# First token chunk's attention output: sums loaded and inverted during groups 10 to 15, projected inside group 15

## The reference

```python
x = x + attn(layernorm(x), wq, wk, wv, wo)
x = x + ffn(layernorm(x), w_router, wg, wu, wd, sg, su, sd)
# attn: 32 query heads of 8, 8 key/value heads; a band of 128 keys below
# the diagonal is masked; softmax over all 1024 keys; out @ wo
# ffn: 8 experts of inner size 640, top 2 per token by sigmoid scores,
# and 2 shared experts of the same size that every token passes
```

## Time and profile before

| what | value |
|---|---|
| median of 3 runs | 960.42 us (959.5 to 963.53) |
| the profiled execution's own time | 959.4 us |
| its span | 957.7 us |
| TensorE busy | 897.4 us (94%) |
| ScalarE busy | 592.1 us (62%) |
| VectorE busy | 445.7 us (47%) |
| chain that ended last | TensorE 75%, ScalarE 9%, VectorE 6% |

### The profile page before, as it was taken

One profiled execution on the slowest core, in us unless ns is written; L12 is line 12 of the kernel. 1 busy time (PEld: TensorE's weight loads), 2 busy tenths in 40 slices (PEclk: granted clock), 3 DMA queues, 4 the chain that ended last, 5 costly groups with the idle time before them and its releaser, 6 DMA issues.

```text
span 957.7 us, 24218 instructions
## 1 busy us (share of the span) xinstructions
PE 897.4 (94%) x8205; PEld 570.2 (60%) x8206; DVE 445.7 (47%) x761; ACT 592.1 (62%) x736; POOL 275.3 (29%) x420
## 2 busy tenths in 40 slices
PE   6959999999999999999997999999999999999994
PEld 4523333333333333333346888888887888888883
DVE  5733334434443344444356767656653434334332
ACT  5769999999999999999982423342212222222221
POOL 4303333232333323333340000000012555444442
PEclk7979999999999999999997999999999999999998
DMA  4350555554444555532112207100027773565421
GB/s 139 105 174 35 179 206 203 196 191 167 148 167 157 205 205 202 196 95 88 31 50 71 66 1 253 38 8 23 1 75 264 259 210 90 160 165 142 143 38 22
DMA packets 41951, 123.67 MB, mean 129 GB/s; under 512 B 7608, under 2 KB 22968, under 8 KB 35760
## 3 DMA queue, kind: packets, MB, share of 16 engines
q1 hardware_dynamic: 30144, 109.37, 33.0%
q0 software_dynamic: 7008, 9.70, 5.7%
q10 hardware_dynamic: 4752, 4.01, 1.3%
HBM read 74.03 MB, written 49.02 MB: 128 GB/s over the span
## 4 chain that ended last, share of the span: by engine, by line
PE 75%; ACT 9%; DVE 6%; issue 5%; SPq 3%; DMA 1%; DVEq 0%; POOL 0%; POOLq 0%; ACTq 0%
PE ps L1618 17%; PE ps L1766 14%; PE ps L1571 13%; PE ps L1720 11%; ACT arena L920 7%; PE ps L1785 7%; PE ps L1733 5%; DVE ps L1118 3%; PE ps L1776 2%; PE ps L1671 1%; PE ps L1525 1%; SPq L529 1%; SPq L526 1%; PE ps L1747 1%; PE ps L1707 1%
## 5 line engine op out<-in xcount | busy, mean ns | idle before, releaser
L920 ACT ACTIVATE arena<-ps 128x1024 f32<-128x1024 f32 x336 | 317.0, 1044 | 5.3 <-PE ps L1571 5.3
L1618 PE MATMUL ps<-arena 128*32 128x256 f32 x4096 | 265.0, 385 | 0.1
L753 POOL TENSOR_SCALAR_AFFINE_SELECT arena<-arena 128x512 f32<-128x512 f32 x240 | 150.0, 638 | 302.0 <-ACT arena L931 202.4
L1571 PE MATMUL ps<-arena 64*128 64x512 bf16 (+1 forms) x1280 | 184.6, 342 | 20.6 <-SPq L568 6.2
L1618 PEld LDWEIGHTS ps<-arena 128*32 128x32 f32 x4096 | 111.8, 109 | 102.9 <-issue 38.2
L1118 DVE COPY_PREDICATED ps<-keep,ps 128x512 f32<-128x512 int32 (+1 forms) x128 | 80.5, 629 | 170.7 <-PE ps L1571 170.7
L1571 PEld LDWEIGHTS ps<-arena 64*128 64x128 bf16 x1280 | 53.6, 94 | 174.7 <-ACT arena L920 83.4
L1766 PE MATMUL ps<-wr_all,x2T 128*128 x648 | 145.7, 366 | 5.5 <-issue 3.5
L1766 PEld LDWEIGHTS ps<-wr_all,x2T 128*128 128x128 f32 x648 | 106.6, 190 | 27.6 <-issue 12.8
L1720 PE MATMUL ps<-x2T,wr_all 128*128 128x512 f32 x480 | 118.5, 398 | 1.2 <-issue 1.2
L931 ACT ACTIVATE arena<-ps 128x1024 f32<-128x1024 f32 x112 | 114.3, 1034 | 8.4 <-DVE ps L1118 3.6
(11 more groups left out here) (188 smaller groups left out, 731.6 us busy)
## 6 DMA issues: line engine op xcount, KB each, us to landing
w_scr<-wr_all SPq DMA_DIRECT2D x24, 1280.0 KB, 7.0
wr_all<-w_scr SPq DMA_DIRECT2D x24, 1280.0 KB, 5.7
raw<-w_experts SPq DMA_DIRECT2D x24, 640.0 KB, 7.1
arena<-q_scr SPq DMA_DIRECT2D x64, 64.0 KB
o_scr<-arena SPq DMA_DIRECT2D x128, 32.0 KB, 1.6
arena<-o_scr SPq DMA_DIRECT2D x16, 256.0 KB, 4.2
raw<-w_shared SPq DMA_DIRECT2D x6, 640.0 KB, 4.4
arena<-q_scr SPq DMA_DIRECT2D x32, 96.0 KB
```

Of the source, the lines that this page charges most:

```text
L753: nc.gpsimd.affine_select(out=dst, in_=src, compare_op=ALU.is_ge if own else ALU.is_gt, fill=0.0, base=0, pattern=[[0, REP], [-1 if own el ...
L920: nc.scalar.activation(prob[:, SLOT[unit(a, kt)], :, :].rearrange("p h q -> p (h q)"), score.rearrange("p b x -> p (b x)"), ACT.Exp, scale ...
L1571: return nc.tensor.matmul(ps[:, bank, :].rearrange("p (h q) -> p h q", h=2)[:, :, place * P:(place + tiles) * P], kst[r0:r0 + HALF, s, kt ...
L1618: last = nc.tensor.matmul(ps[32 * h:32 * h + 32, 6 + qc, a % 2 * QW:(a % 2 + 1) * QW], vst[:, s, kt, :], prob[:, SLOT[k], h, :], start=(no ...
```

## The change

`load_sums(0)` is issued after SP's part of group 10. Piece i of the inversion is put into VectorE's group 11 + i, between `merge_pair` 1 and `merge_pair` 2, and `normalize(0)` into group 15 at the same place. TensorE projects the first half of chunk 0 after score blocks 26 and 27 of group 15, into bank 6, and the second half after block 28, into the banks that block 26 has left; the value blocks of the last turns come behind. VectorE adds and takes each half's statistics as it comes, and writes the normalized rows to `xnc_first`, a place in the buffer that held the attention weights. The transposed rows of chunk 0 go to banks 4 and 5.

```diff
+XT_BANK = (4, 6, 6, 6)
+FIRST_O = (6, 2 * BUF[NEXP - 3])
...
@@ SP @@
-            for n in range(2 * LOOPED, NG - 1):
-                group_io(n, n % 2, n < SPLIT_PAIRS, n + 1 < NG - 1, n + 2 < NG)
-
...
-            sp.wait_ge(o_stored[0], 16 * REP * KV + FIRST)
-            load_sums(0)
-            group_io(NG - 1, 1, False, False, False)
+            for n in range(2 * LOOPED, NG):
+                group_io(n, n % 2, n < SPLIT_PAIRS, n + 1 < NG - 1, n + 2 < NG)
+                if n == 2 * LOOPED:
+                    sp.wait_ge(o_stored[0], 16 * REP * KV + FIRST)
+                    load_sums(0)
...
@@ VectorE @@
-            def group(g, s, more):
+            def group(g, s, more, also=lambda: None):
 
                 merge_pair(g, 1)
+                also()
                 merge_pair(g, 2)
...
+            for n in range(2 * LOOPED, NG - 1):
+                i = n - 2 * LOOPED - 1
+                group(n, n % 2, n + 2 < NG, (lambda: invert(0, i)) if 0 <= i < INVERT else (lambda: None))
+
+            def add_first(half):
+
+                dve.wait_ge(c_proj, half + 1 + FIRST)
+                for t in range(2 * half, 2 * half + 2):
+                    nc.vector.tensor_tensor(x_rows(0, t), x_rows(0, t), ps[:, FIRST_O[half], t % 2 * D:(t % 2 + 1) * D],
+                                            ALU.add) \
+                        .then_inc(c_added, 1)
+                for t in range(2 * half, 2 * half + 2):
+                    dve.wait_ge(c_added, t + 1)
+                    nc.vector.bn_stats(stats[:, t, :], x_rows(0, t)).then_inc(dve_step, 1)
+
+            def first_rows():
+
+                layernorm(dve, lambda t: x_rows(0, t), lambda t: xnc_first[:, t, :], first_base, INVERT, c_xn, NC + 1, False)
...
             merge_pair(NG - 1, 1)
-            invert(0, 0)
-            invert(0, 1)
+            normalize(0)
             merge_pair(NG - 1, 2)
             acc_out(NG - 1, 0)
             merge_pair(NG - 1, 3)
-            invert(0, 2)
-            invert(0, 3)
-            normalize(0)
+            add_first(0)
+            add_first(1)
+            first_rows()
             acc_out(NG - 1, 1)
-            new_rows(0)
             xT_copy(0)
             ahead_of(-1)
...
@@ TensorE @@
-            for t in range(1, len(TURNS)):
-                turn_of(NG - 1, 1, NG // 2 - 1, t, True, False)
-            for v in TURNS[0][1]:
-                if len(v) == 3:
-                    values(NG - 1, 1, unit(*v[0:2]))
-            pe.wait_ge(acc_free, 2 + NG * QC - 1)
...
+            LAST_MERGE = max(t for t, (products, _) in enumerate(TURNS) if (QP - 1, 1) in products)
+            last = (NG - 1, 1, NG // 2 - 1)
+            for t in range(1, LAST_MERGE + 2):
+                turn_of(*last, t, True, False)
+            products_of(*last, LAST_MERGE + 2, False)
+            pe.wait_ge(c_oT, 1)
+            pe.wait_ge(merged, NG * NMERGE)
+            project(0, range(0, 2))
+            products_of(*last, LAST_MERGE + 3, False)
+            pe.wait_ge(s_free, NG * NEXP - 2 + BUFS)
+            project(0, range(2, 4))
+            for t in range(LAST_MERGE + 2, len(TURNS)):
+                if t > LAST_MERGE + 3:
+                    products_of(*last, t, False)
+                values_of(*last, t, True)
+            for v in TURNS[0][1]:
+                if len(v) == 3:
+                    values(NG - 1, 1, unit(*v[0:2]))
```

More of the change, by code:

```diff
@@ L355, in build @@
         raw = at("raw", [P, 2, BW], F32, 2 * WSLOT + top[0])
+        xnc_first = arena[:, top[0]:top[0] + TPC * D].rearrange("p (t d) -> p t d", d=D)
+        assert top[0] + TPC * D <= 2 * WSLOT
         carve(2 * BW)
@@ L417, in build @@
         y_free, now_ix = sem("y_free"), sem("now_ix")
+        c_added = sem("c_added")
         shift_low, shift_high = sem("shift_low"), sem("shift_high")
@@ L442, in wait_apart, with layernorm @@
             eng.sem_inc(apart, 1)
-        def layernorm(eng, src, dst, base, n0, xn_done, round_):
+        def layernorm(eng, src, dst, base, n0, xn_done, round_, sums=True):
             n = n0
             for t in range(TPC):
-                nc.vector.bn_stats(stats[:, t, :], src(t)).then_inc(dve_step, 1)
+                if sums:
+                    nc.vector.bn_stats(stats[:, t, :], src(t)).then_inc(dve_step, 1)
                 n += 1
@@ L936, in x2_out @@
                 for k in range(KD):
-                    nc.scalar.copy(x2T[:, 0, k, ds(c * CT, CT)], ps[:, 6 + k, :]).then_inc(c_xT, 1)
-                act.dma_start(xn_scr[ds(c * CT, CT), :].rearrange("(t p) d -> p t d", p=P), xnc).then_inc(c_kept, 16)
+                    nc.scalar.copy(x2T[:, 0, k, ds(c * CT, CT)], ps[:, XT_BANK[c] + k, :]).then_inc(c_xT, 1)
+                act.dma_start(xn_scr[ds(c * CT, CT), :].rearrange("(t p) d -> p t d", p=P), xnc if c else xnc_first) \
+                    .then_inc(c_kept, 16)
             def shared(c):
@@ L1162, in _ @@
                     group(it * 2 + s, s, True)
-            for n in range(2 * LOOPED, NG - 1):
-                group(n, n % 2, n + 2 < NG)
             def x_rows(c, t):
@@ L1180, in normalize @@
             def normalize(c):
-                dve.wait_ge(dve_step, c * C_DVE + (first_base + INVERT))
+                dve.wait_ge(dve_step, c * C_DVE + (first_base - (TPC if c else 0) + INVERT))
                 nc.vector.tensor_tensor(numer, numer, denom, ALU.mult).then_inc(c_oT, 1)
+            for n in range(2 * LOOPED, NG - 1):
+                i = n - 2 * LOOPED - 1
+                group(n, n % 2, n + 2 < NG, (lambda: invert(0, i)) if 0 <= i < INVERT else (lambda: None))
+            assert NG - 2 * LOOPED - 2 == INVERT
+            def add_first(half):
[9 more added lines that the diff above has]
+                layernorm(dve, lambda t: x_rows(0, t), lambda t: xnc_first[:, t, :], first_base, INVERT, c_xn, NC + 1, False)
             def new_rows(c):
@@ L1192, in new_rows @@
                     n += 1
-                dve.wait_ge(dve_step, c * C_DVE + (first_base + n))
+                dve.wait_ge(dve_step, c * C_DVE + (first_base - TPC + n))
                 wait_apart(dve, c_kept, c * 16 + FIRST)
-                n = layernorm(dve, lambda t: x_rows(c, t), lambda t: xnc[:, t, :], c * C_DVE + first_base, n, c_xn,
+                n = layernorm(dve, lambda t: x_rows(c, t), lambda t: xnc[:, t, :], c * C_DVE + (first_base - TPC), n, c_xn,
                               c + (NC + 1))
@@ L1201, in xT_copy @@
                 dve.wait_ge(c_xT, c * KD + KD)
-                nc.vector.tensor_tensor(x2T[:, 1, :, ds(c * CT, CT)], ps[:, 6:8, :],
+                turned_rows = ps[:, XT_BANK[c]:XT_BANK[c] + KD, :]
+                nc.vector.tensor_tensor(x2T[:, 1, :, ds(c * CT, CT)], turned_rows,
                                         x2T[:, 0, :, ds(c * CT, CT)].bitcast(F32), ALU.subtract).then_inc(c_xlo, 1)
-                nc.vector.tensor_copy(xTc, ps[:, 6:8, :]).then_inc(c_xTc, 1)
+                nc.vector.tensor_copy(xTc, turned_rows).then_inc(c_xTc, 1)
             def logits_out(c):
@@ L1252, in _ @@
             merge_pair(NG - 1, 3)
-            invert(0, 2)
-            invert(0, 3)
-            normalize(0)
+            add_first(0)
+            add_first(1)
+            first_rows()
             acc_out(NG - 1, 1)
-            new_rows(0)
             xT_copy(0)
             ahead_of(-1)
-            base += NC * C_DVE
+            base += NC * C_DVE - TPC
             count = [base]
@@ L1621, in values, with products_of @@
                 last.then_inc(p_free, 1)
-            def turn_of(n, s, turn, t, before, after):
-                products, ended = TURNS[t]
-                for p in products:
+            def products_of(n, s, turn, t, after):
+                for p in TURNS[t][0]:
                     if not isinstance(p, int):
@@ L1632, in turn_of, with values_of @@
                         scores(n + 1, 1 - s, turn + s, ISSUE_NO[p - NEXP])
-                for v in ended:
+            def values_of(n, s, turn, t, before):
+                for v in TURNS[t][1]:
                     if len(v) == 2:
@@ L1637, in turn_of @@
                         values(n - 1, 1 - s, unit(*v[0:2]))
+            def turn_of(n, s, turn, t, before, after):
+                products_of(n, s, turn, t, after)
+                values_of(n, s, turn, t, before)
             def group(n, s, turn):
@@ L1656, in _, with project @@
             group(NG - 2, 0, NG // 2 - 1)
-            for t in range(1, len(TURNS)):
-                turn_of(NG - 1, 1, NG // 2 - 1, t, True, False)
-            for v in TURNS[0][1]:
-                if len(v) == 3:
-                    values(NG - 1, 1, unit(*v[0:2]))
-            pe.wait_ge(acc_free, 2 + NG * QC - 1)
[L1664 to L1669, removed]
+            def project(c, tiles):
+                for t in tiles:
+                    bank = 6 + t // 2 if c else FIRST_O[t // 2]
                     for k in range(KD):
```

(14 more changed lines are left out.)

## The result

| | median | runs | ratio to before |
|---|---|---|---|
| before | 961.52 us | 6 (957.04 to 964.01) | |
| changed | 968.83 us | 6 (966.8 to 971.7) | 1.0082, 95% interval 1.006 to 1.0105 |

The changed kernel is slower by 7.3 us.

A forecast was written before the change was run, and what follows sets the result against it. It took attention to be bound by two full engines, TensorE and ScalarE, with room on VectorE. Terms 11.4 + 2.6 - 7.0 = +7.0 us gave a median of 967.0 us, range 962 to 971.5.

The forecast's parts named there:

- The signs that it named: Expected in the profile: loads near 381, about 13 us VectorE idle in group 11, then clock 0.50 for some 6 us.
- Term 1: Group 11: VectorE's inversion waits for late sums, delaying merge_pair 2 and stalling TensorE and ScalarE: +11.4 us, bounds 10.0 and 12.3.
- Term 2: Group 11 after the stall: TensorE's clock drops to half for 6.4 us of dense work: +2.6 us, between 0.4 and 3.2.
- rival (b): Stall stands, but ScalarE hides the slow clock (+0.4) and chunk 1's sums are in time (8.6): 963.6 us, chance 0.13.
- Term 3: End of group 15 and handoff to the shared experts get shorter: -7.0 us, bounds 5.5 and 8.6.
- the second wait: After the handoff, VectorE waits for the sums of chunk 1, so shared_up 2 loses 1.6 us.
- Rival (c): Projection in group 15 holds up score block 28 and the values; handoff gains only 0.97: +13.0, 973.4 us, chance 0.08.
- Rival (a): Group 11: sums arrive in time (first issue by 369.6), no stall or slow clock, handoff won: 953.4 us, chance 0.07.
- The side effect that was put at nothing: Group 15: normalize meeting a mask would cost GpSimd 0.8 us of its idle time, nothing for the sum.

The follow-up runs named there:

- r1: The changed kernel, unaltered, run again beside r2 and r3 on one chip: 968.65 us, ratio 1.0087 to the kernel before.
- e1: Changed kernel, but SP issues load_sums(0) in front of its part of group 10, not behind it: 954.38 us, ratio 0.9942 to the kernel before.
- e2: Changed kernel, SP as it is, but inversion piece i in group 12 + i, the last with normalize(0) in group 15: 956.82 us, ratio 0.9974 to before.
- e6: Changed kernel, but load_sums(0) issued inside load_pair(12), behind 6 of its 14 transfers: 963.91 us, ratio 1.0037 to the kernel before.
- e7: Changed kernel, but load_sums(0) issued inside load_pair(12), behind 12 of its 14 transfers: 965.83 us, ratio 1.0063 to the kernel before.
- r2: The kernel of e1 run again beside r1 and r3: 954.99 us, ratio 0.9946 to the kernel before.
- e5: e1, but in group 15 SP issues the sums of chunk 1 between the two accumulators' stores: 954.50 us, ratio 0.9936 to the kernel before.
- r3: The kernel of e5 run again beside r1 and r2: 953.43 us, ratio 0.9928 to the kernel before.

## Why the prediction was right

The forecast was 967.0 us in 962 to 971.5, slower; measured 968.83. The signs that it named are all in the traces; only the clock of 0.50 behind the stall lasted 4.1 us in the profiled execution, 6.1 in r1, where some 6 was named. By its terms:

**Term 1, +11.4.** Measured 11.1 in the trace (the 0.3 are in the landing: 6.3 us from first issue to landing, 6.57 taken). e1 removes it by issuing earlier, e2 by asking later, e6 and e7 shorten it. That both full engines would stand is in the brackets 11.51 and 11.16.

**Term 2, +2.6.** Measured 1.6 in the profiled execution and 2.5 in r1, inside the bounds of 0.4 and 3.2. The price was right, 2.6 over 6.4 us or 0.41 for a microsecond at the low clock, against about 0.4 in six traces, though 2.6 was chosen between two bounds and not worked out. What varies between executions is how long the clock stays low. ScalarE did not hide the slow clock, so rival (b) is out in this part.

**Term 3, -7.0.** Measured 13.2 - 8.0 = 5.2. The step up to the first shared product was right: 6.75 gained, 6.8 forecast. Up to the second it was 8.45 against 8.6. The mis-sized part is the second wait, put at 1.6 us and measured at 2.57: the four stores took 2.62 us to the first load (517.39 to 520.01) and not 1.75, and the loads 7.0 us and not 6.57. ScalarE issued the transfer of chunk 0's rows (512 KB) at 517.69, beside these stores; that it slowed them is not shown. Another 0.5 went between the third shared product and the projection of chunk 1 (7.5 to 8.0 us behind), where TensorE waited 0.16 us for `normalize(1)`. Rival (c) is out: block 28 was up in time, and nothing waited around the projection.

**The sum.** +7.0 forecast; 11.1 + 1.6 - 5.2 = +7.5 along the trace; +7.3 between the medians. That these are so close is in part luck: terms 1 and 2 were 0.3 and 1.0 too high here, and the gain of term 3 was 1.8 too high the other way. In r1 terms 1 and 2 made 13.6 of the 14.0 forecast, and the distance to the kernel before was 8.9 us. The medians of the experiments say the same: 13.7 to 14.3 us for the late sums, and 4.8 (r2) to 5.6 us (e1) for the rest, of 7.0. So it is term 3 that was over-sized, by 1.4 to 2.2 us. Of the 1.8 us between 967.0 and 968.83, 1.1 is the kernel before, at 961.52 in six runs and 960.42 in the three of the forecast. The profiled execution is 971.7 us, the slowest of the six, 12.3 over the one profiled before. The 4.3 us that no term names stand behind chunk 1, where this execution had the low clock for some 7 us near 695 and 3 us near 730, the one before for 3 us near 720; how much of the 4.3 us that is has not been worked out.

**Rival (a)**: between it and the forecast stood one reading, that SP reaches the loads only at 381. e1 has what it described, with the first issue at 355 where 369.6 was to decide: 954.38 us against its 953.4, with a gain of 5.6 us and not 7.0 over its own kernel before.

The side effect that was put at nothing was nothing here (the multiplication ran at 495.09, before the masks at 496.65), and cost 0.85 us of TensorE in e2.

## What to carry to other kernels

An operation moved ahead brings its wait along. Before it is put into an in-order queue in front of something that the busiest engine needs, find the time at which its input lands, from the issuing queue's own timeline: here one place in SP's order was worth 14 us, more than twice what the rest of the change gained. A gap of 3.8 us holds 1.75 us of work but no wait. Asking later (e2) removed the wait as loading earlier (e1) did, but it filled the gap in the last group and ended 2.4 us behind. And when a phase is shortened, look at what the next phase's first load was hidden behind.

## What the runs showed of the hardware

Behind a pause of TensorE of 7 to 11 us the clock cost 1.3 to 2.6 us, and no less behind 7 us than behind 11. What differed, in one and the same program too, was how long the clock stayed at 0.50 after TensorE had started again: 3.4 to 6.2 us, at about 0.4 us of time for each.

A shorter wait can end either way. TensorE's wait for the sums of chunk 1 was followed by 3.4 to 3.5 us of low clock in e1, e2 and e7 (waits of 2.40, 2.83 and 2.61 us), and by none in the changed kernel, r1, r2 and e6 (2.57, 2.54, 2.42 and 2.52 us). In e1 the 12 matmuls behind it took 4.62 us, in r2 3.03. The length of the wait alone doesn't decide it.

Much of the scatter between executions goes with the clock as well: over the 23, 12 and 13 executions of the kernel before that stand beside the experiments, time and mean granted clock correlate at -0.82, -0.59 and -0.95. The profile page's row of the granted clock in 40 slices, for e5 and then for r3, the same kernel:

```profile
PEclk7979999999999999999999999999999999999998
```
```profile
PEclk8969999999999999999999999999899999999997
```

Summed over windows of 5 us from 60 us on, the clock was low for about 16 us in e5 (span 949.6) and 32 in r3 (952.5); 19 in e1 (952.8) and 33 in r2 (956.6); 43 in the changed kernel's first profile (970.0) and 34 in r1 (967.9). For e5 and r3, and for e1 and r2, most of the difference lies in two pauses, near 680 and 715, in the routing, which every variant has, and some in the last 15 us, where TensorE has little work left. That the low clock makes the longer times, and not only goes with them, is shown here for group 11 alone. Differences of 3 us between single executions of this kernel therefore say nothing about an edit.
